# Top-k attention on one core: scores issued right behind the turned tiles, sums by transposes, and ScalarE's exponentials ahead of its evacuation

## The chip, the cores and the metric

One core of one Trainium2 chip runs the whole program. The metric is the device time in microseconds (us), the median of several executions. Five engines work side by side, each on its own list of instructions in order, and semaphores tie them together: TensorE (PE in the profile, its weight loads PEld), VectorE (DVE), ScalarE (ACT), GpSimd (POOL) and SyncE (SP, which starts the DMAs).

## The reference, cut to what matters

```python
# x: 32 batches of 256 tokens x 128 channels; 16 heads of 8 channels
xn = layernorm(x)
q, k, v = heads(xn @ Wqkv.T + bqkv)
q, k = layernorm(q, q_gamma, q_beta), layernorm(k, k_gamma, k_beta)
scores = q @ k.T / sqrt(8)                      # 256 x 256 for each head
aw = softmax(scores)
aws = aw * (aw >= 12th largest of the row)      # topk = int(256 * 0.05)
o_s = (aws / (aws.sum(-1) + 1e-8)) @ v
qf, kf = softmax(q), softmax(k)                 # over the 8 channels
o_l = qf @ (kf.T @ v) / (qf @ kf.sum(tokens) + 1e-6)
o = a * o_s + (1 - a) * o_l                     # a = sigmoid(alpha), one for each head
y = x + o @ Wproj.T + bproj + xn @ W[idx] + b[idx]
```

## The kernel before, in words

**Passes, slots and tiles.** The loop `iterations` makes 34 passes, `it` from -2 to 31, and in a steady pass works on several batches at once. A pass has eight slots, `u_` from 0 to 7, one for each unit of two heads. A unit has four tiles of 128 rows x 256 keys. "Slot 5" below is what an engine's list holds for `u_ == 5`.

**One unit's way.** PE writes a unit's scores into `score_ps` (two buffers) one slot ahead, in `scores(u_)`, for unit u+1. In slot u, DVE finds each row's eight largest (`top`, `largest`), POOL takes the largest away from them (`drop`), and ACT makes the exponentials of the four tiles (`e`, line 879, each followed by a read of the accumulator) and of the eight largest (`e8`, line 884). In slot u+1 DVE replaces those eight in `e` (`remove`, line 661, into `rest`) and finds the next eight (`following`, line 667, `next8`). In slot u+2 POOL and ACT make the masks `below` (POOL three tiles or four, ACT the rest, line 892). In slot u+4 PE turns the eight half tiles: one transpose of `e` and one product with `minus_huge` for each, sixteen instructions into `turn_ps` (`turn`, lines 1051 and 1052). ACT evacuates `turn_ps` with a Relu into `kept` (line 839). Every second slot PE multiplies two units' `kept` by the values (`product`, into `pv_ps`).

**Single buffers.** `turn_ps` is one buffer: `turn(u_)` waits until `kept` of the slot before has been made (`turn_copied`). `work_ps` and `pv_ps` are one bank each and pass through many hands: `work_ps` through qfT, kv, lin, the turned q and k (`w_qkT`), their two remainders (`part`, three bf16 parts), the values (`w_v`, line 1144), the turned xn and the projections q and k (`w_qk`, line 1156); `pv_ps` through the products, the sums, the turned output and the output projection (lines 1128 to 1131).

**Sums.** `sums()` in slot 5 of PE brings the 8 channels and the row's sum of each head together: `oT` (ACT's copy of the products, 32 rows for each head) is the stationary operand and `gather`, 36 columns of zeros and ones, the moving one, eight times; each of these fp32 products is two instructions in the trace. Then `eps_ident` times `z` adds 1e-8 of the full sum, once for each half of the tokens. ACT copies the result in slot 5 (line 908).

**The order in a slot** is written out by hand on every engine. On PE: `turn`, `product` (even slots), `sums` (slot 5), `early`, `scores`, `late`. `early` holds the qfT transposes (slot 0), the turned output (1), the output projection (3), the second remainder (5), the values (6) and w_qk (7). `late` holds kv (1), lin (2), w_qkT (3), the first remainder (4) and the turned xn (6). On ACT: `kept`, then the copies that others wait for (slot 1 rsqrt, 3 lin, 4 the first part, 6 `v_aug`, 7 `over_rec`), the exponentials with `e8`, the masks of two units earlier, and the other copies (0 and 4 `oT`, 4 and 5 the further parts, 7 `qk_sq` and `qk_raw`). On POOL, `drop` is first in a slot; behind it come the steps of q and k's normalisation and the masks.

Of the kernel before, what the change touches and what calls it, by code (L numbers as in the profile page):

```python
# [84 lines left out]
def build(nc, x, Wqkv, bqkv, q_gamma, q_beta, k_gamma, k_beta, alpha, Wproj, bproj, W, bW, logits, u, y):  # L85
# [15 lines left out]
    with ExitStack() as ctx:  # L101
# [13 lines left out]
        gather = sb("gather", [P, 4 * VA])  # L115
# [169 lines left out]
        def _(pool):  # L285
# [24 lines left out]
            used = gather[:].rearrange("p (j e) -> p j e", e=VA)  # L310
            select(used, ALU.not_equal, 1.0, 0, [[-VW, 4], [-1, VA]], 1, 7).then_inc(s["gather_ready"], 1)
            select(minus_one[:], ALU.not_equal, -1.0, 0, [[-1, P]], 1, 8).then_inc(s["gather_ready"], 1)
# [466 lines left out]
        def _(act):  # L779
# [48 lines left out]
            def body(it, par, xr):  # L828
                nxt = 1 - par
                for u_ in range(UNITS):  # L830
# [4 lines left out]
                    if exists(it if u_ >= 4 else it - 1):  # L835

                        wait(act, s["pv_ready"], it * QUADS + (u_ - 8) // 2 + 1)
                        act.wait_ge(s["turn_ready"], g - 3)
                        nc.scalar.activation(kept[:, u_ % 4], turn_ps[:], ACT.Relu).then_inc(s["turn_copied"], 1)  # L839
# [9 lines left out]
                    if u_ == 1 and exists(it - 2):  # L849
                        act.wait_ge(s["w_osT"], it - 1)  # L850
                        nc.scalar.copy(osT[:], pv_ps[:, 0:N]).then_inc(s["osT_copied"], 1)
# [34 lines left out]
                    if exists(it if u_ >= 2 else it - 1):  # L886

                        r = (u_ - 2) % RING
                        act.wait_ge(s["next_ready"], TILES * (g - 1))
                        for t in range(POOL_TILES[r], TILES):  # L890

                            nc.scalar.activation(below[:, r, t, :], e[:, r, t, :], ACT.Relu, scale=-1.0,  # L892
                                                 bias=next8[:, r, t, TOPK - 9:TOPK - 8]).then_inc(s["below_act"], 1)


# [9 lines left out]
                    if u_ == 5 and exists(it - 1):  # L905
                        act.wait_ge(s["w_turn"], it)
                        wait(act, s["osp_ready"], it - 1)
                        nc.scalar.copy(sums_sb.rearrange("p g e -> p (g e)"), pv_ps[:, 0:NT * H * VA]).then_inc(  # L908
                            s["sums_copied"], 1)
                    if u_ == 0 and exists(it):  # L910
# [40 lines left out]
                    if u_ == 7 and exists(it + 2):  # L951
# [5 lines left out]
                        nc.scalar.copy(qk_raw[:], work_ps[:]).then_inc(s["raw_ready"], 1)  # L957
                    if (it, u_) == (-2, 7):
# [403 lines left out]
```

## Time and profile before

| | us |
|---|---|
| median of 3 runs | 1219.39 |
| lowest, highest | 1219.28, 1228.09 |
| the profiled execution, its own time | 1222.3 |
| its span in the profile | 1220.5 |
| DVE busy in the span | 1151.5 |
| ACT busy | 1065.0 |
| PE busy | 1011.5 |
| POOL busy | 995.2 |

The span is from the first to the last instruction of the profiled execution; its own time is what the device took for it. The profiler's granted clock of PE has two levels here, 1.00 (2.4 GHz) and 0.50 (1.2 GHz), and its mean over the span is 0.962. An engine's busy time says how much work it has; what holds the end is seen from the waits of the engine with the most work.

### The profile page before, as it was taken

To read this page: it belongs to the slowest core of one execution; us is meant where nothing else is said; L and a number is where in the kernel's file an instruction comes from. 1 tells how busy PE (TensorE), PEld (TensorE's weight loads), DVE (VectorE), ACT (ScalarE), POOL (GpSimd) and SP (SyncE) were. 2 spreads that over 40 slices of the span, in tenths; PEclk is the share of its full clock that TensorE was granted. 3 is DMA by queue.
4 is the path that set the end of the run, shared out by engine and by line. 5 is a ranking of instruction groups with operands and counts; after the bars stand their busy time and mean duration, and the time that the engine had idled before them with its cause. 6 is when DMAs were issued, how large, how long until landed. Compare 5 with 4: busy or idle time off the path is not lost.

```text
span 1220.5 us, 34803 instructions
## 1 busy us (share of the span) xinstructions
PE 1011.5 (83%) x9381; PEld 707.2 (58%) x9412; DVE 1151.5 (94%) x4358; ACT 1065.0 (87%) x3474; POOL 995.2 (82%) x1972
## 2 busy tenths in 40 slices
PE   4578888888888888888888888888888888888888
PEld 1356556656556556556655656656556655656655
DVE  6999999999999999999999999999999999999994
ACT  3689898999989899998899989899989898989884
POOL 5688888888888888888888888888888888888863
PEclk9989999999999899999999999899999999999988
DMA  3122222122222122222122222122222122222110
GB/s 101 42 65 66 84 83 79 37 67 70 84 83 83 37 62 70 84 84 84 36 68 65 84 84 83 37 62 71 83 84 82 38 72 61 84 79 79 44 46 10
DMA packets 165126, 82.79 MB, mean 68 GB/s; under 512 B 7737, under 2 KB 164927, under 8 KB 164930
## 3 DMA queue, kind: packets, MB, share of 16 engines
q1 hardware_dynamic: 164658, 80.43, 22.8%
q8 instruction: 77, 1.26, 0.4%
q14 instruction: 119, 0.97, 0.3%
q10 hardware_dynamic: 272, 0.13, 0.0%
HBM read 42.78 MB, written 37.75 MB: 66 GB/s over the span
## 4 chain that ended last, share of the span: by engine, by line
POOL 32%; PE 27%; ACT 19%; issue 15%; DVE 5%; DMA 1%; DVEq 0%; POOLq 0%; ACTq 0%; SPq 0%
ACT e L879 12%; POOL gap L437 10%; POOL below L441 5%; PE turn_ps L1051 5%; PE pv_ps L1073 3%; POOL qkn L359 3%; PE work_ps L1156 3%; POOL qk_b L359 3%; PE pv_ps L1084 3%; DVE top L654 3%; PE turn_ps L1052 2%; POOL drop L412 2%; PE work_ps L1144 2%; PE work_ps L1187 2%; POOL sq_half L422 2%
## 5 line engine op out<-in xcount | busy, mean ns | idle before, releaser
L879 ACT ACTIVATE e<-score_ps,drop 128x256 f32<-128x256 f32 x1024 | 475.2, 495 | 31.1 <-POOL drop L412 30.9
L1051 PE MATMUL turn_ps<-ident,e 128*128 128x128 f32 x2016 | 401.9, 293 | 21.0 <-ACT part L863 17.5
L661 DVE MATCH_REPLACE8 rest<-e 128x256 f32<-128x256 f32 x1020 | 415.9, 412 | 0.0
L667 DVE MAX8 next<-rest 128x8 f32<-128x256 f32 x1020 | 410.4, 419 | 0.5 <-issue 0.3
L654 DVE MAX8 top<-score_ps 128x8 f32<-128x256 f32 x1024 | 362.0, 419 | 34.4 <-PE score_ps L1033 34.1
L1052 PE MATMUL turn_ps<-minus_huge,below 128*128 128x128 bf16 x2016 | 380.0, 226 | 0.0
L437 POOL TENSOR_SCALAR gap<-e,next 128x256 bf16<-128x256 f32 x794 | 368.9, 479 | 0.0
L1051 PEld LDWEIGHTS turn_ps<-ident,e 128*128 128x128 f32 x2016 | 296.8, 147 | 59.3 <-issue 21.7
L839 ACT ACTIVATE kept<-turn_ps 128x1024 f32<-128x1024 f32 x252 | 267.5, 1062 | 56.9 <-PE turn_ps L1052 56.9
L441 POOL TENSOR_SCALAR below<-gap 128x768 bf16<-128x768 bf16 (+1 forms) x254 | 216.7, 853 | 41.4 <-POOL gap L437 41.4
L879 ACT ACTIVATION_READ_ACCUMULATOR e<-score_ps,drop 128x1 f32 x1024 | 232.9, 227 | 0.0
L1052 PEld LDWEIGHTS turn_ps<-minus_huge,below 128*128 128x128 bf16 x2016 | 222.3, 110 | 0.7
L412 POOL TENSOR_TENSOR drop<-top 128x36 f32<-128x36 f32 x256 | 62.8, 245 | 132.0 <-DVE top L654 117.7
L1073 PE MATMUL pv_ps<-kept,v_aug 128*32 128x256 f32 x2000 | 142.2, 404 | 2.9 <-ACT over L908 2.2
L892 ACT ACTIVATE below<-e,next 128x256 bf16<-128x256 f32 x222 | 120.1, 541 | 0.0
L1033 PE MATMUL score_ps<-k_slots,q_slots 64*128 64x256 bf16 x1024 | 105.1, 283 | 11.8 <-issue 5.4
L661 DVE MATCH_VALUE_LOAD rest<-e 128x8 f32 x1020 | 80.1, 79 | 15.5 <-ACT e L884 15.4
L1084 PE MATMUL pv_ps<-gather,oT 128*128 128x36 f32 x496 | 61.7, 281 | 32.8 <-ACT oT L901 32.8
L1073 PEld LDWEIGHTS pv_ps<-kept,v_aug 128*32 128x32 f32 x2000 | 55.4, 114 | 50.2 <-issue 31.7
L1084 PEld LDWEIGHTS pv_ps<-gather,oT 128*128 128x128 f32 x496 | 58.1, 192 | 39.8 <-ACT oT L901 39.8
L1033 PEld LDWEIGHTS score_ps<-k_slots,q_slots 64*128 64x128 bf16 x1024 | 30.7, 95 | 69.3 <-issue 60.7
L884 ACT ACTIVATE e<-drop 128x32 f32<-128x32 f32 x256 | 67.2, 263 | 0.0
(229 smaller groups left out, 1439.6 us busy)
## 6 DMA issues: line engine op xcount, KB each, us to landing
part_slots<-part SPq DMA_DIRECT2D x128, 192.0 KB, 2.3
q_slots<-part_slots SPq DMA_DIRECT2D x64, 256.0 KB, 3.5
k_slots<-part_slots SPq DMA_DIRECT2D x64, 256.0 KB, 4.2
part_slots<-part SPq DMA_DIRECT2D x64, 128.0 KB, 1.9
x_sb<-in_L_attn_x SPq DMA_DIRECT2D x32, 128.0 KB, 4.0
x_res<-in_L_attn_x SPq DMA_DIRECT2D x32, 128.0 KB, 4.2
out_y<-out_sb SPq DMA_DIRECT2D x32, 128.0 KB, 4.4
w_ops<-in_L_ffn_W SPq DMA_DIRECT2D x1, 512.0 KB
```

The lines of the kernel that those rows point to most:

```text
L437: nc.gpsimd.tensor_scalar(gap[:, half, t, :], e[:, r, t, :], -1.0, next8[:, r, t, TOPK - 9:TOPK - 8], ALU.mult, ALU.add).then_inc(s["gap_s ...
L441: nc.gpsimd.tensor_scalar(below[:, r, 0:many], gap[:, half, 0:many], HUGE, 0.0, ALU.min, ALU.max).then_inc(s["below_pool"], many)
L654: nc.vector.max(top[:, q, t, 1:9], score_ps[:, q, t // 2, t % 2, :]).then_inc(s["top_ready"], 1)
L661: nc.vector.match_replace(rest[:, t, :], e8[:, (u_ - 1) % 2, t, :], e[:, (u_ - 1) % RING, t, :], REMOVED).then_inc(s["rest_ready"], 1)
L667: nc.vector.max(next8[:, (u_ - 1) % RING, t, :], rest[:, t, :]).then_inc(s["next_ready"], 1)
L839: nc.scalar.activation(kept[:, u_ % 4], turn_ps[:], ACT.Relu).then_inc(s["turn_copied"], 1)
L879: nc.scalar.activation(e[:, u_ % RING, t, :], score_ps[:, u_ % 2, t // 2, t % 2, :], ACT.Exp, bias=drop[:, u_ % 2, t, 0:1], accum_out=z[:, ...
L1033: last = mm(score_ps[:, v_ % 2, hh, nt, :], q_slots[rows, side, v_, nt * P:(nt + 1) * P], k_slots[rows, side, v_, :], start=True, stop=True)
L1051: mm(dst, e[:, r, t, keys], ident[:], start=True, stop=False, is_transpose=True)
L1052: last = mm(dst, below[:, r, t, keys], minus_huge[:], start=False, stop=True)
L1073: last = mm(pv_ps[32 * j:32 * (j + 1), half * N:(half + 1) * N], v_aug[:, side, mc, 4 * q + j, :], kept[:, v_ % 4, j % 2, mc, :], start=(m ...
L1084: mm(pv_ps[:, at:at + 4 * VA], oT[:, nxt, q // 2, 1 - q % 2, t * P:(t + 1) * P], gather[:], start=(t == 0 and q == 0), stop=False, skip_gr ...
```

## The change

Four edits, all in the order or the form of work; nothing else differs.

1. `sums()` becomes eight transposes with a permutation: `gather` grows from 36 to 128 columns, the spare 92 columns pick rows of `oT` that hold zeros, and the product with `gather` is issued with `is_transpose`. The two products with `eps_ident` (16 columns each) become one of 32. The tail's own sums change alike. POOL makes one more `affine_select` in the set-up.
2. PE's order in a slot: `scores` stands right behind `turn`, save that `product` stays ahead of it in slots 0 and 4, and `early` in slots 3, 5 and 6. `product` of slots 2 and 6, `sums`, and `early` of slots 0, 1 and 7 now come behind `scores`.
3. ACT's `kept` (with its wait for `turn`) moves behind the slot's exponentials and `e8`, and the copy of `osT` behind it. ACT's lines shift: exponentials 873, `e8` 878, `kept` 884.
4. ACT's masks `below` move from behind the exponentials to the end of the slot (line 956).

```diff
-        gather = sb("gather", [P, 4 * VA])
+        gather = sb("gather", [P, P])
...
-            used = gather[:].rearrange("p (j e) -> p j e", e=VA)
+            used = gather[:, 0:4 * VA].rearrange("p (j e) -> p j e", e=VA)
+            spare = gather[:, 4 * VA:].rearrange("p (j e) -> p j e", e=VW - VA)
             select(used, ALU.not_equal, 1.0, 0, [[-VW, 4], [-1, VA]], 1, 7).then_inc(s["gather_ready"], 1)
+            select(spare, ALU.not_equal, 1.0, -VA, [[-VW, 4], [-1, VW - VA]], 1, 7).then_inc(s["gather_ready"], 1)
...
-                    if exists(it if u_ >= 4 else it - 1):
-
-                        wait(act, s["pv_ready"], it * QUADS + (u_ - 8) // 2 + 1)
-                        act.wait_ge(s["turn_ready"], g - 3)
-                        nc.scalar.activation(kept[:, u_ % 4], turn_ps[:], ACT.Relu).then_inc(s["turn_copied"], 1)
...
                         nc.scalar.activation(e8[:, u_ % 2], drop[:, u_ % 2, :, 1:9], ACT.Exp).then_inc(s["e8_ready"], 1)
 
-                    if exists(it if u_ >= 2 else it - 1):
-
-                        r = (u_ - 2) % RING
-                        act.wait_ge(s["next_ready"], TILES * (g - 1))
-                        for t in range(POOL_TILES[r], TILES):
-
-                            nc.scalar.activation(below[:, r, t, :], e[:, r, t, :], ACT.Relu, scale=-1.0,
-                                                 bias=next8[:, r, t, TOPK - 9:TOPK - 8]).then_inc(s["below_act"], 1)
-
-
+                    if exists(it if u_ >= 4 else it - 1):
+
+                        wait(act, s["pv_ready"], it * QUADS + (u_ - 8) // 2 + 1)
+                        act.wait_ge(s["turn_ready"], g - 3)
+                        nc.scalar.activation(kept[:, u_ % 4], turn_ps[:], ACT.Relu).then_inc(s["turn_copied"], 1)
...
                         for q in range(QUADS):
                             at = (t * QUADS + q) * 4 * VA
-                            mm(pv_ps[:, at:at + 4 * VA], oT[:, nxt, q // 2, 1 - q % 2, t * P:(t + 1) * P], gather[:],
-                               start=(t == 0 and q == 0), stop=False, skip_group_check=True)
+                            mm(pv_ps[:, at:at + P], oT[:, nxt, q // 2, 1 - q % 2, t * P:(t + 1) * P], gather[:],
+                               start=(t == 0 and q == 0), stop=False, is_transpose=True, skip_group_check=True)
...
-                    for t in range(NT):
-                        over_t = pv_ps[:, t * H * VA:(t + 1) * H * VA].rearrange("p (h e) -> p h e", e=VA)[:, :, D]
-                        last = mm(over_t, eps_ident[:], z[:, nxt, t, :], start=False, stop=True, skip_group_check=True)
-                    last.then_inc(s["w_turn"], 1)
+                    mm(pv_ps[:, 0:NT * H * VA].rearrange("p (g e) -> p g e", e=VA)[:, :, D], eps_ident[:],
+                       z[:, nxt].rearrange("p t h -> p (t h)"), start=False, stop=True,
+                       skip_group_check=True).then_inc(s["w_turn"], 1)
...
                     if exists(it if u_ >= 4 else it - 1):
                         turn(u_)
-                    if u_ % 2 == 0 and exists(it if u_ >= 6 else it - 1):
+                    if u_ in (0, 4) and exists(it - 1):
                         product(u_)
+                    if u_ in (3, 5, 6) or u_ == 7 and it < 0:
+                        early(u_)
+                    if exists(it if u_ < UNITS - 1 else it + 1):
+                        scores(u_)
+                    if u_ in (2, 6) and exists(it if u_ >= 6 else it - 1):
+                        product(u_)
+                    if u_ == 0 or u_ == 7 and it >= 0:
+                        early(u_)
                     if u_ == 5 and exists(it - 1):
                         sums()
-                    early(u_)
-                    if exists(it if u_ < UNITS - 1 else it + 1):
-                        scores(u_)
                     late(u_)
+                    if u_ == 1:
+                        early(u_)
```

ACT, slots 1 to 3 of a steady pass, before: `kept` stands ahead of each slot's exponentials. The first row is the end of slot 1, the last one the end of slot 3's exponentials.

```order
L892 ACTIVATE below<-e,next 128x256
L839 ACTIVATE kept<-turn_ps 128x1024
L879 ACTIVATE e,z<-score_ps,drop 128x256 x4
L884 ACTIVATE e<-drop 128x32
L892 ACTIVATE below<-e,next 128x256
L839 ACTIVATE kept<-turn_ps 128x1024
L857 COPY over<-work_ps 128x288
L879 ACTIVATE e,z<-score_ps,drop 128x256 x4
L884 ACTIVATE e<-drop 128x32
```

The same stretch of the changed kernel, from the end of slot 1:

```order
L956 ACTIVATE below<-e,next 128x256
L873 ACTIVATE e,z<-score_ps,drop 128x256 x4
L878 ACTIVATE e<-drop 128x32
L884 ACTIVATE kept<-turn_ps 128x1024
L956 ACTIVATE below<-e,next 128x256
L851 COPY over<-work_ps 128x288
L873 ACTIVATE e,z<-score_ps,drop 128x256 x4
L878 ACTIVATE e<-drop 128x32
L884 ACTIVATE kept<-turn_ps 128x1024
```

Slot 2's `kept`, which stood ahead of slot 2's exponentials and of their wait for `drop`, now stands behind them.

PE, the end of slot 5's `turn` to the start of slot 6's, before:

```order
L1052 MATMUL turn_ps<-minus_huge,below 128x128
L1084 MATMUL pv_ps<-gather,oT 128x36 x8
L1090 MATMUL pv_ps<-z,eps_ident 128x16 x2
L1097 MATMUL work_ps<-part,minus_one 128x512
L1033 MATMUL score_ps<-k_slots,q_slots 128x256 x4
L1051 MATMUL turn_ps<-ident,e 128x128
```

and of the changed kernel:

```order
L1052 MATMUL turn_ps<-minus_huge,below 128x128
L1096 MATMUL work_ps<-part,minus_one 128x512
L1033 MATMUL score_ps<-k_slots,q_slots 128x256 x4
L1084 MATMUL pv_ps<-gather,oT 128x128 x8
L1088 MATMUL pv_ps<-z,eps_ident 128x32
L1051 MATMUL turn_ps<-ident,e 128x128
```

The sums, half as many instructions and wider ones, moved behind the scores; the remainder (`minus_one`) stays ahead of them.

PE, the end of slot 6's `turn` to the start of slot 7's, before:

```order
L1052 MATMUL turn_ps<-minus_huge,below 128x128
L1073 MATMUL pv_ps<-kept,v_aug 32x256 x8
L1144 MATMUL work_ps<-w_v,xnT 128x128
L1145 MATMUL work_ps<-bias,ones 128x128
L1144 MATMUL work_ps<-w_v,xnT 128x128
L1145 MATMUL work_ps<-bias,ones 128x128
L1033 MATMUL score_ps<-k_slots,q_slots 128x256 x4
L1213 MATMUL work_ps<-ident,xn 128x128 x2
```

and of the changed kernel:

```order
L1052 MATMUL turn_ps<-minus_huge,below 128x128
L1143 MATMUL work_ps<-w_v,xnT 128x128
L1144 MATMUL work_ps<-bias,ones 128x128
L1143 MATMUL work_ps<-w_v,xnT 128x128
L1144 MATMUL work_ps<-bias,ones 128x128
L1033 MATMUL score_ps<-k_slots,q_slots 128x256 x4
L1073 MATMUL pv_ps<-kept,v_aug 32x256 x8
L1212 MATMUL work_ps<-ident,xn 128x128 x2
```

The product moved behind the scores; the values stay ahead of them.

## Rows read from the trace of the kernel before

**Rows 1.** Stretches, one a pass: length; busy PE, PEld, DVE, ACT, POOL; PE's clock

```profile
30.98:66.72 35.74, 21.06 (x146) 13.27 (x148) 34.85 (x131) 25.56 (x95) 25.42 (x51) 1.00 0.21 61
...
615.58:651.02 35.44, 29.99 (x296) 21.35 (x295) 35.07 (x135) 33.02 (x109) 30.69 (x61) 1.00 0.23 66
...
1125.58:1163.01 37.43, 29.47 (x284) 20.77 (x283) 34.95 (x132) 33.71 (x111) 30.38 (x59) 0.93 0.25 71
```

**Rows 2.** Who waited for whom: us in total, times, longest us

```profile
ACT kept L839 <- PE turn_ps L1052: 56.9, 58, 7.3
DVE top L654 <- PE score_ps L1033: 34.1, 33, 5.5
DVE rest L661 <- ACT e L884: 15.4, 31, 0.6
```

**Rows 3.** DVE in time order: start us, us, line, operation [idle before]

```profile
610.66 1.43 DVE L654 MAX8 top<-score_ps 128x8 f32<-128x256 f32 x4 [0.99 <-PE score_ps L1033]
612.68 0.09 DVE L661 MATCH_VALUE_LOAD rest<-e 128x8 f32 x1 [0.59 <-ACT e L884]
...
624.50 1.41 DVE L654 MAX8 top<-score_ps 128x8 f32<-128x256 f32 x4
...
633.72 1.42 DVE L654 MAX8 top<-score_ps 128x8 f32<-128x256 f32 x4
...
637.92 1.42 DVE L654 MAX8 top<-score_ps 128x8 f32<-128x256 f32 x4
...
646.33 1.42 DVE L654 MAX8 top<-score_ps 128x8 f32<-128x256 f32 x4
```

**Rows 4.** Stretches with one slot's turned tiles alone, `turn_ps`, columns as in rows 1

```profile
604.80:607.75 2.95, 2.82 (x16) 2.02 (x16) 0.00 (x0) 0.00 (x0) 0.51 0.03 7
641.50:643.30 1.80, 1.59 (x16) 1.28 (x16) 0.00 (x0) 0.00 (x0) 1.00 0.02 6
```

**Rows 5.** PE in time order, turned tiles left out

```profile
601.98 1.98 PE L1084 MATMUL pv_ps<-gather,oT 128*128 128x36 f32 x16 [1.07 <-ACT oT L901]
...
610.08 0.40 PE L1033 MATMUL score_ps<-k_slots,q_slots 64*128 64x256 bf16 x4
...
628.93 0.44 PE L1128 MATMUL pv_ps<-x_res,ident 128*128 128x128 f32 x2
...
631.12 0.40 PE L1033 MATMUL score_ps<-k_slots,q_slots 64*128 64x256 bf16 x4
...
644.37 0.49 PE L1144 MATMUL work_ps<-w_v,xnT 128*128 128x128 f32 x2
...
645.52 0.40 PE L1033 MATMUL score_ps<-k_slots,q_slots 64*128 64x256 bf16 x4
```

**Rows 6.** ACT in time order, accumulator reads left out

```profile
616.29 0.65 ACT L953 ACTIVATE qk_sq<-work_ps 128x512 f32<-128x512 f32 x1
...
627.10 0.47 ACT L879 ACTIVATE e<-score_ps,drop 128x256 f32<-128x256 f32 x1 [0.50 <-POOL drop L412]
...
629.03 0.52 ACT L892 ACTIVATE below<-e,next 128x256 bf16<-128x256 f32 x1
629.43 1.03 ACT L839 ACTIVATE kept<-turn_ps 128x1024 f32<-128x1024 f32 x1
...
640.46 0.51 ACT L879 ACTIVATE e<-score_ps,drop 128x256 f32<-128x256 f32 x1
```

**Rows 7.** POOL in time order

```profile
617.39 0.73 POOL L422 TENSOR_TENSOR sq_half<-qk_sq 128x256 f32<-128x256 f32 x1
...
626.82 0.25 POOL L412 TENSOR_TENSOR drop<-top 128x36 f32<-128x36 f32 x1
```

**Rows 8.** Stretches, `work_ps` alone: w_qk of slot 7, columns as in rows 1

```profile
648.50:650.35 1.85, 1.75 (x6) 0.78 (x6) 0.00 (x0) 0.00 (x0) 1.00 0.99 263
```

**Rows 9.** Stretches, `pv_ps` alone: slot 1's four transposes; the sums (no DVE column)

```profile
621.20:622.00 0.80, 0.63 (x4) 0.42 (x4) 0.00 (x0) 1.00 0.00 0
638.70:641.20 2.50, 2.41 (x20) 2.31 (x20) 0.00 (x0) 1.00 0.40 123
```

More of the change, by code:

```diff
@@ L848, in body @@
                             s["over_ready"], 1)
-                    if u_ == 1 and exists(it - 2):
-                        act.wait_ge(s["w_osT"], it - 1)
-                        nc.scalar.copy(osT[:], pv_ps[:, 0:N]).then_inc(s["osT_copied"], 1)
                     if u_ == 1 and (exists(it + 1) or exists(it + 2)):
@@ L909, in body @@
                             s["sums_copied"], 1)
+                    if u_ == 1 and exists(it - 2):
+                        act.wait_ge(s["w_osT"], it - 1)
+                        nc.scalar.copy(osT[:], pv_ps[:, 0:N]).then_inc(s["osT_copied"], 1)
                     if u_ == 0 and exists(it):
@@ L957, in body @@
                         nc.scalar.copy(qk_raw[:], work_ps[:]).then_inc(s["raw_ready"], 1)
+                    if exists(it if u_ >= 2 else it - 1):
+                        r = (u_ - 2) % RING
+                        act.wait_ge(s["next_ready"], TILES * (g - 1))
+                        for t in range(POOL_TILES[r], TILES):
+                            nc.scalar.activation(below[:, r, t, :], e[:, r, t, :], ACT.Relu, scale=-1.0,
+                                                 bias=next8[:, r, t, TOPK - 9:TOPK - 8]).then_inc(s["below_act"], 1)
                     if (it, u_) == (-2, 7):
@@ L1152, in early @@
                             pe.wait_ge(s["pool_const"], 7)
-                            pe.wait_ge(s["gather_ready"], 3)
+                            pe.wait_ge(s["gather_ready"], 4)
                         for t in range(NT):
@@ L1321, in _ @@
             sums_ps = turn_ps[:, 0].rearrange("p m n -> p (m n)")
-            for t in range(NT):
-                over_t = sums_ps[:, t * H * VA:(t + 1) * H * VA].rearrange("p (h e) -> p h e", e=VA)[:, :, D]
-                mm(over_t, eps_ident[:], z[:, side, t, :], start=(t == 0), stop=False, skip_group_check=True)
+            mm(sums_ps[:, 0:NT * H * VA].rearrange("p (g e) -> p g e", e=VA)[:, :, D], eps_ident[:],
+               z[:, side].rearrange("p t h -> p (t h)"), start=True, stop=False, skip_group_check=True)
             for q in range(QUADS):
@@ L1328, in _ @@
                     at = (t * QUADS + q) * 4 * VA
-                    last = mm(sums_ps[:, at:at + 4 * VA], oT[:, side, q // 2, 1 - q % 2, t * P:(t + 1) * P], gather[:],
-                              start=False, stop=(q == QUADS - 1), skip_group_check=True)
+                    last = mm(sums_ps[:, at:at + P], oT[:, side, q // 2, 1 - q % 2, t * P:(t + 1) * P], gather[:],
+                              start=False, stop=(q == QUADS - 1), is_transpose=True, skip_group_check=True)
             last.then_inc(s["w_turn"], 1)
```

## The prediction

> **What bounds the kernel now.** I read the stretches of whole passes first. A pass here runs from DVE's first `top` of slot 0 to the next pass's. There are 31 of them, from 30.98 to 1163.01 us, so 36.52 us each on average [rows 1]. In the pass at 615.58 DVE is busy for 35.07 of 35.44 us: VectorE is the bound, and the rest of a pass is what DVE waits for. The clock column splits the passes in two kinds. Twelve of the 31 show 1.00, eight of those last 35.4 to 35.8 us and the longest 36.5; the other nineteen show 0.95 or less and last 36.3 to 38.5. Then the waits: in the whole run DVE waits 34.1 us for scores, once a pass, and 15.4 us for `e8`, 0.5 a pass [rows 2]. So 1.6 us a pass is all that a better order can remove, 49.5 us or 4% of the run, unless VectorE's own work shrinks, which the change leaves alone.
>
> Where are the waits? In the pass before the one at 615.58, at the start of slot 7: `top` waits 0.99 us for scores that ended at 610.48, and then `remove` 0.59 us for `e8` [rows 3, 5]. Ahead of this PE ran at half clock: slot 6's turned tiles took 2.82 us there against 1.59 us a pass later at full clock [rows 4], and in that later pass `top` of slot 7 started at 646.33 with no wait in its row [rows 3]. In seventeen of the nineteen passes the clock falls 2.1 to 4.1 us into slot 5, during or just behind the sums, which PE reaches after 1.07 us of idle time [rows 5], and comes back 3.4 us later, or 6.8 in three passes. So the waits for scores are mostly the price of the clock.
>
> **The sums.** Before, slot 5's sums take 2.41 us for 20 instructions [rows 9], all ahead of the scores for slot 6. Eight transposes with 128 columns are nearest to slot 1's four, which take 0.63 us with the tail of the last [rows 9]: about 1.1 us, and 0.2 us for the one product with `eps_ident`. As half of the instructions go, 2.41 us is the dear end and 1.1 the cheap one; I take 1.3. Neither is on DVE's path, since the sums now stand behind the scores and ACT's copy of them waits for `kept` anyway. What they may change is the clock. What PE does before it falls is the idle stretch and the narrow sums. Where it does a slot's turned tiles around an idle stretch, the clock holds, and turned tiles are themselves half transposes of 128 columns, as the new sums are. So I expect the clock to hold. A fall now costs more, see below.
>
> The Trainium skill speaks against this. "TensorE: Matmul & The Clock Gate", Part 4 on the PE-mode transpose, says that transposes do not count as busy for the clock. The trace rather disagrees, as the turned tiles are half transposes and keep 1.00. By that rule the falls would stay or spread, which is the second rival.
>
> **The scores behind the turned tiles.** In slots 6 and 2 the product (1.1 us) no longer stands ahead of the scores, in slot 5 the sums, in slot 0 qfT, in slot 1 the turned output, in slot 7 w_qk (1.75 us, [rows 8]). All of it is time by which scores could come earlier, if nothing else holds the turned tiles that stand in front of them.
>
> **`kept` behind the exponentials.** This is what holds them. `turn_ps` is one buffer, so slot u+1's turned tiles wait for slot u's `kept`. Before, `kept` waited for PE alone, and PE was the slower of the two (56.9 us of ACT waiting for turned tiles [rows 2]). Now `kept` also waits for slot u's exponentials, these for `drop`, this for DVE's `top`. This closes a loop over two slots: `top` of slot u, `drop`, exponentials, `kept`, `turn` of u+1, what stands between it and the scores, scores, `top` of slot u+2. Every time round it must fit into DVE's two slots. Its steps:
>
> - exponentials start 0.03 us after `drop`'s end (626.82+0.25, then 627.10), and the next ACT instruction behind `e8` starts 1.93 us later (629.03) [rows 6, 7];
> - `kept` takes 1.03 us [rows 6], the turned tiles 1.59 at full clock [rows 4], the scores 0.40 [rows 5]; from their end to `top` it is 0.18 us (610.48 to 610.66) [rows 3, 5]. For ACT to PE I estimate 0.05, and -0.15 for each group of PE that starts before the one ahead has ended.
>
> *Slot 2 to slot 4.* `drop` ends 2.57 us after slot 2's `top` starts (627.07-624.50), as POOL is behind there. Between `turn` and scores stands the output projection: 2.19 us from its start to the scores' (631.12-628.93) [rows 5]. Sum 2.57+0.03+1.93+1.03+0.05+1.59+2.19+0.40+0.18-0.15 = 9.8 us, against the 9.22 from `top` to `top` (633.72-624.50) [rows 3]: 0.6 us of new waiting at slot 4's `top`.
>
> *POOL on top of it.* w_qk is now behind slot 7's scores, so `qk_sq` (0.65 us, [rows 6]) ends at the earliest 1.75+0.65-0.2 = 2.2 us after slot 0's `top`. `sq_half` started at +1.81 before (617.39, `top` at 615.58) [rows 1, 7] and moves by 0.4. From there to slot 4 POOL has hardly a gap, so slot 2's `drop` comes up to 0.4 us later. Bounds 0 and 0.4; I take 0.4, as POOL is continuously at work there.
>
> *Slot 5 to slot 7.* Slot 4's work on ACT is the same sum in another order, so slot 5's exponentials start where they did, 2.54 us after `top` (640.46-637.92) [rows 3, 6]. Between `turn` and scores stand the values, 1.15 us (645.52-644.37) [rows 5]. Sum 2.54+1.93+1.03+0.05+1.59+1.15+0.40+0.18-0.15 = 8.7 us against 8.41 (646.33-637.92): 0.3 us at slot 7's `top`. `v_aug` and the exponentials of slot 6 wait for the same values, so `e8` is late by the full 0.59 us in every pass, as in each pass in which `top` waits now [rows 3].
>
> The other slots have no work between `turn` and scores or only 1.1 us (slot 4's product), and the same sum gives 7 to 8.3 us in 8.4 to 9 us. They have 0.1 to 1 us to spare, so I add 0.1 for the tightest, slot 1.
>
> **The masks** at the end of a slot are turned two slots later, and hold only ACT: nothing. The new `affine_select` stands in the first 31 us, where POOL waits for loads: nothing, at most the half microsecond that it takes. The tail saves some of its sums, below half a microsecond.
>
> **The sum.** A pass becomes 35.07 of DVE's work + 0.6 + 0.4 + 0.3 + 0.6 + 0.1 = 37.1 us, 0.55 more than the mean of 36.52, over some 30 passes +17 us. From the profiled execution (span 1220.5, own time 1222.3) that gives 1239, from the median of 1219.39, which is 3 us lower than that execution, **1236 us**. Each wait is a difference of two large sums, so its error is a few tenths: 0.5 us a pass either way is 15 us, and the forecast's own range is 1222 to 1250.
>
> **Rivals.** *The loop does not bind.* If `kept` is in time, because the chain from slot 2's `drop` to slot 4's `top` takes 9.2 us or less and the one of slot 5 8.4 or less, and the clock holds, every pass is one of 35.44 us or a little less: 1219-30x1.08 = 1187 us. For it: my two overruns are only 0.3 and 0.6 us, and waits shift other waits. Against it: `drop` of slot 2 is late by its own engine. It decides at about half a microsecond in each chain.
>
> *The clock still falls.* In nineteen of 31 passes, behind the sums. Then slot 6's turned tiles cost 2.82-1.59 = 1.23 us more, now fully on the loop, and the values a little, 1.4 together: 0.61x1.4x30 = 26 us on top of the forecast, 1262. If it falls in every pass, 1278. For it: PE has less work and more idle time, about 1 us ahead of most slots' turned tiles. Against it: slot 5's sums are as wide as turned tiles.
>
> *A draw.* The clock's gain and the loop's loss cancel: the waits move to other slots, passes last 36.5 us, 1219.
>
> **Chances.** The forecast 0.45, the loop does not bind 0.20, the clock falls 0.18, a draw 0.17. A change of 1% (1207 to 1232) is about what a measurement can tell from none. Of the forecast's 0.45 about 0.13 lies below 1232. Same: 0.13+0.15 and 0.02 of the first rival: 0.30. Faster: 0.18 and 0.02: 0.20. Slower: 0.32+0.18: 0.50. The range runs from 1190, next to the first rival, which keeps about half of its chance in, to 1266, with most of the second.
>
> **What the changed profile would show.** Right: DVE's `top` in slot 4 waits for scores behind the output projection, a wait that is not there now; PE's turned tiles wait for ACT's `kept` in most slots, where now ACT waits for PE; `e8` is waited for about 0.6 us a pass; PE's clock is near 1.00 in the steady passes. Wrong: waits for scores under 10 us in the whole run (then the loop does not bind), or clock falls behind slot 5's sums as before.

## The result, and the profile after

| | median us | lowest, highest | ratio to before, 95% interval |
|---|---|---|---|
| before, beside the changed kernel | 1221.86 | 1219.28, 1228.09 | |
| changed | 1251.56 | 1248.48, 1253.95 | 1.0234 [1.0185, 1.0283] |

The change makes the kernel 2.3% slower, about 30 us. The profiled execution took 1252.17 us and its span is 1250.3, against 1222.3 and 1220.5 before. The mean granted clock rose from 0.962 to 0.981, and yet the time rose.

The page of the changed kernel, its span, parts 1 and 2 (PE's clock in 40 slices), and the group of the moved `kept` from part 5:

```profile
span 1250.3 us, 34136 instructions
...
PE 952.4 (76%) x9061; PEld 657.8 (53%) x9092; DVE 1157.6 (93%) x4358; ACT 1074.7 (86%) x3474; POOL 1001.3 (80%) x1973
...
PEclk9989999999999999999999999999999999999998
...
L884 ACT ACTIVATE kept<-turn_ps 128x1024 f32<-128x1024 f32 x252 | 264.0, 1048 | 2.4 <-PE turn_ps L1052 2.4
```

DVE has the same 4358 instructions and nearly the same busy time (1157.6 us; 1151.5 before), PE is busy for 59 us less. So no engine has notably more to do; DVE waits more. The last number in `kept`'s row is the idle time ahead of it: 2.4 us in the whole run, where before it waited 56.9 us for turned tiles [rows 2]. ACT is hardly ever early with `kept` any more.

Stretches of single passes of the changed kernel, columns as in [rows 1]:

```profile
69.25:105.85 36.60, 26.38 (x266) 17.96 (x268) 35.24 (x135) 31.63 (x104) 30.56 (x61) 1.00 0.21 60
632.95:670.16 37.21, 28.75 (x284) 20.07 (x285) 35.44 (x135) 32.88 (x106) 30.63 (x61) 1.00 0.26 73
670.16:707.17 37.01, 28.78 (x284) 20.06 (x285) 35.34 (x136) 33.41 (x109) 31.09 (x62) 1.00 0.24 70
481.52:520.28 38.76, 30.16 (x284) 20.78 (x285) 35.47 (x135) 34.55 (x112) 31.59 (x62) 0.96 0.22 61
707.17:745.77 38.60, 28.84 (x284) 20.08 (x285) 35.36 (x136) 34.75 (x112) 31.54 (x62) 1.00 0.23 66
1157.36:1195.42 38.06, 29.60 (x281) 20.33 (x281) 35.04 (x131) 33.73 (x111) 30.27 (x58) 0.96 0.24 67
```

Nine of the thirty passes behind the first last 37.01 to 37.03 us, as the third row: that is the forecast's 37.1. But the mean of the thirty is (1195.42-69.25)/30 = 37.54, against 36.54 before ((1163.01-66.72)/30, [rows 1]): +1.00 a pass, 30 us in all. The first pass takes 38.41 us against 35.74, the tail 2.6 less; these two cancel. There are two kinds of longer passes: with a fall of the clock (0.96 in the fourth and the last row, nine passes), and with full clock and a long last slot (38.60, fifth row).

Who waited for whom in the changed kernel, us in total, times, longest:

```profile
PE turn_ps L1051 <- ACT kept L884: 255.0, 181, 2.4
...
DVE top L656 <- PE score_ps L1033: 49.8, 58, 2.7
...
DVE rest L663 <- ACT e L878: 18.3, 31, 0.6
...
PE score_ps L1033 <- issue: 8.5, 13, 1.5
```

PE now stands 255 us in front of turned tiles for `kept`; before, the wait ran the other way. DVE waits 49.8 us for scores (34.1 before, [rows 2]) and 18.3 for `e8` (15.4). The last row is the one that my prediction had no word for: PE stands at scores and "issue" names no releaser. The same view of the kernel before had it too, smaller:

```profile
PE score_ps L1033 <- issue: 5.4, 7, 1.2
```

The pass at 632.95, DVE in time order: `top` of slots 2, 3, 4, 5 and 7.

```profile
641.89 1.40 DVE L656 MAX8 top<-score_ps 128x8 f32<-128x256 f32 x4
...
652.15 1.61 DVE L656 MAX8 top<-score_ps 128x8 f32<-128x256 f32 x4 [0.96 <-PE score_ps L1033]
...
656.56 1.41 DVE L656 MAX8 top<-score_ps 128x8 f32<-128x256 f32 x4
...
665.18 1.43 DVE L656 MAX8 top<-score_ps 128x8 f32<-128x256 f32 x4
```

PE in the same pass, slot 3: turned tiles, output projection, scores.

```profile
647.98 0.30 PE L1051 MATMUL turn_ps<-ident,e 128*128 128x128 f32 x1 [0.70 <-ACT kept L884]
...
649.37 0.44 PE L1127 MATMUL pv_ps<-x_res,ident 128*128 128x128 f32 x2
...
651.57 0.40 PE L1033 MATMUL score_ps<-k_slots,q_slots 64*128 64x256 bf16 x4
```

ACT, slot 2 of the pass:

```profile
644.87 0.47 ACT L873 ACTIVATE e<-score_ps,drop 128x256 f32<-128x256 f32 x1 [0.63 <-POOL drop L414]
...
646.69 0.24 ACT L878 ACTIVATE e<-drop 128x32 f32<-128x32 f32 x1
646.81 1.03 ACT L884 ACTIVATE kept<-turn_ps 128x1024 f32<-128x1024 f32 x1
```

POOL, `qk_sq`'s half in slot 0 and `drop` of slot 2:

```profile
635.16 0.73 POOL L424 TENSOR_TENSOR sq_half<-qk_sq 128x256 f32<-128x256 f32 x1 [0.34 <-ACT qk_sq L945]
...
644.59 0.25 POOL L414 TENSOR_TENSOR drop<-top 128x36 f32<-128x36 f32 x1
```

Read as a chain: `top` 641.89, `drop` ends 644.84, exponentials to `e8`, `kept` 646.81 to 647.84, turned tiles from 647.98, scores from 651.57, `top` 652.15. That is 10.26 us from `top` to `top`, where DVE's own work took 9.22 before [rows 3].

Now the last slot of the long pass at 707.17. SP's queue, start and length of the issue, PE, and DVE's `top` of the next pass's slot 0:

```profile
740.78 0.36 SPq L272 DMA_DIRECT2D q_slots<-part_slots  x1
741.19 0.50 SPq L272 DMA_DIRECT2D k_slots<-part_slots  x1
```

```profile
742.11 0.30 PE L1051 MATMUL turn_ps<-ident,e 128*128 128x128 f32 x1 [1.72 <-ACT kept L884]
...
745.19 0.40 PE L1033 MATMUL score_ps<-k_slots,q_slots 64*128 64x256 bf16 x4 [1.53 <-issue]
```

```profile
745.77 0.43 DVE L656 MAX8 top<-score_ps 128x8 f32<-128x256 f32 x1 [1.56 <-PE score_ps L1033]
```

These scores are unit 0 of the next batch. Its q and k come through DRAM: ACT's third part (its copy ends at 736.76, 0.68 us from 736.08) is written out by SP, and when the writes have landed SP reads them back, q at 740.78 and k at 741.19. The reload takes 3.3 and 3.9 us from issue to landing (medians of 64). So k lands near 745.1, and PE, with the turned tiles done, stands 1.53 us for it. In thirteen of thirty passes PE waits here. What varies from pass to pass is mostly the write leg: the last write, issued 0.5 us behind the copy, lands 1.9 to 2.0 us after its issue in seventeen passes and 2.6 to 3.7 us after it in the other thirteen, and twelve of the thirteen waits follow such a late landing. Why it is late there was not looked into.

The clock of the changed kernel: slot 2 of the pass at 481.52, and the longest stretch without a fall.

```profile
492.45:495.87 3.42, 3.42 (x28) 2.11 (x30) 2.73 (x11) 2.79 (x11) 3.42 (x6) 0.50 0.00 0
495.87:1055.60 559.73, 429.70 (x4225) 299.53 (x4232) 527.74 (x1999) 498.06 (x1610) 462.74 (x911) 1.00 0.24 69
```

For 560 us, some fifteen passes and as many sums, the clock holds 1.00. It falls in nine passes, in slot 2, behind the turned output and an idle stretch in front of turned tiles, as PE's row just ahead of the fall shows (the idle time in brackets):

```profile
492.28 0.30 PE L1051 MATMUL turn_ps<-ident,e 128*128 128x128 f32 x1 [1.14 <-ACT kept L884]
```

### The profile page after: what moved, and what is told of

Read it like the earlier page. It is cut to its first block, busy times and chain, and to the rows that moved or that the text cites. A ratio compares the mean times of both kernels' runs of the same rounds, so it can differ in the third digit from the quotient of the medians.

```text
span 1250.3 us, 34136 instructions
## 1 busy us (share of the span) xinstructions
PE 952.4 (76%) x9061; PEld 657.8 (53%) x9092; DVE 1157.6 (93%) x4358; ACT 1074.7 (86%) x3474; POOL 1001.3 (80%) x1973
## 4 chain that ended last, share of the span: by engine, by line
ACT 37%; PE 31%; POOL 16%; issue 11%; DVE 5%; DVEq 0%; DMA 0%; POOLq 0%; ACTq 0%; SPq 0%
ACT e L873 18%; ACT kept L884 10%; PE turn_ps L1051 10%; POOL gap L439 5%; PE turn_ps L1052 4%; PE work_ps L1155 3%; POOL below L443 3%; DVE top L656 3%; PE score_ps L1033 2%; PE pv_ps L1130 2%; PE work_ps L1143 2%; POOL qk_a L355 2%; POOL drop L414 2%; ACT oT L890 1%; ACT qk_exp L915 1%
## 5 line engine op out<-in xcount | busy, mean ns | idle before, releaser
L1051 PE MATMUL turn_ps<-ident,e 128*128 128x128 f32 x2016 | 389.6, 287 | 255.1 <-ACT kept L884 255.0
L1051 PEld LDWEIGHTS turn_ps<-ident,e 128*128 128x128 f32 x2016 | 289.8, 144 | 310.3 <-issue 217.5
L656 DVE MAX8 top<-score_ps 128x8 f32<-128x256 f32 x1024 | 361.9, 415 | 53.8 <-PE score_ps L1033 49.8
L669 DVE MAX8 next<-rest 128x8 f32<-128x256 f32 x1020 | 405.7, 413 | 0.5 <-issue 0.3
L1052 PE MATMUL turn_ps<-minus_huge,below 128*128 128x128 bf16 x2016 | 369.5, 223 | 0.0
L873 ACT ACTIVATION_READ_ACCUMULATOR e<-score_ps,drop 128x1 f32 x1024 | 223.2, 218 | 0.0
L1052 PEld LDWEIGHTS turn_ps<-minus_huge,below 128*128 128x128 bf16 x2016 | 217.3, 108 | 0.0
L1073 PE MATMUL pv_ps<-kept,v_aug 128*32 128x256 f32 x2000 | 136.3, 391 | 0.0
L663 DVE MATCH_VALUE_LOAD rest<-e 128x8 f32 x1020 | 74.6, 73 | 18.3 <-ACT e L878 18.3
L861 ACT COPY v_aug<-work_ps 128x256 f32<-128x256 f32 x32 | 11.9, 373 | 51.6 <-PE work_ps L1144 51.6
L1155 PE MATMUL work_ps<-w_qk,xnT 128*128 128x256 f32 x128 | 46.9, 449 | 0.9 <-ACT xnT L942 0.9
```

The costliest lines, as they stand in the source:

```text
L656: nc.vector.max(top[:, q, t, 1:9], score_ps[:, q, t // 2, t % 2, :]).then_inc(s["top_ready"], 1)
L663: nc.vector.match_replace(rest[:, t, :], e8[:, (u_ - 1) % 2, t, :], e[:, (u_ - 1) % RING, t, :], REMOVED).then_inc(s["rest_ready"], 1)
L669: nc.vector.max(next8[:, (u_ - 1) % RING, t, :], rest[:, t, :]).then_inc(s["next_ready"], 1)
L873: nc.scalar.activation(e[:, u_ % RING, t, :], score_ps[:, u_ % 2, t // 2, t % 2, :], ACT.Exp, bias=drop[:, u_ % 2, t, 0:1], accum_out=z[:, ...
L1051: mm(dst, e[:, r, t, keys], ident[:], start=True, stop=False, is_transpose=True)
L1052: last = mm(dst, below[:, r, t, keys], minus_huge[:], start=False, stop=True)
```

## The experiments

"Per pass" is the mean of the thirty passes behind the first in the profiled execution, 36.54 us before and 37.54 changed. The ratio is always to the kernel before.

### The halves of the change

**ACT's new order alone**, on the kernel before (`kept` and the `osT` copy behind the exponentials, masks at the end of the slot):

```diff
-                    if exists(it if u_ >= 4 else it - 1):    # kept, ahead of the slot's copies and exponentials
...
                         nc.scalar.activation(e8[:, u_ % 2], drop[:, u_ % 2, :, 1:9], ACT.Exp)...
+                    if exists(it if u_ >= 4 else it - 1):    # kept, behind e8
```

> The kernel before with ScalarE's new order alone (kept behind the exponentials, masks last); TensorE's order and the sums as before. Theory 1: the same loop now also holds the sums (2.4 us), the products, the turned output and w_qk between turned tiles and scores, so slots 4 to 6, 6 to 0 and 0 to 2 overrun too: a pass of 39 us or more, 1290 to 1340 us. Theory 2 (loop harmless): within 1% of the kernel before or of the changed one, under 1255 us.

Measured 1359.63 us, 1.1115 [1.1083, 1.1146], 40.84 us a pass. Its waits:

```profile
PE turn_ps L1049 <- ACT kept L882: 245.9, 166, 3.1
...
DVE top L654 <- PE score_ps L1031: 153.7, 125, 3.3
```

The loop through `kept` binds wherever `early`, a product or the sums still stand between turned tiles and scores: four waits for scores a pass instead of one. 3.0 us a pass fall on `top` of slot 0 alone, behind w_qk. This half by itself costs 11%, more than the 1290 to 1340 us expected.

**The short sums alone**, on the kernel before:

```diff
+                            mm(pv_ps[:, at:at + P], oT[:, nxt, q // 2, 1 - q % 2, t * P:(t + 1) * P], gather[:],
+                               start=(t == 0 and q == 0), stop=False, is_transpose=True, skip_group_check=True)
...
+                    mm(pv_ps[:, 0:NT * H * VA].rearrange("p (g e) -> p g e", e=VA)[:, :, D], eps_ident[:],
+                       z[:, nxt].rearrange("p t h -> p (t h)"), start=False, stop=True,
```

> The kernel before with the short sums alone (eight transposes of 128 columns and one product with eps_ident). If the wide transposes hold TensorE's clock: no falls in slot 5, mean granted clock over 0.985, passes of 35.4 to 35.8 us, about 1190 us. If transposes do not hold it: clock near 0.96 as before and 1205 to 1220 us, only the instruction time gained.

Measured 1199.83 us, 0.9804 [0.9773, 0.9834], 36.08 us a pass. Page and waits:

```profile
PE 961.2 (80%) x9092; PEld 659.2 (55%) x9092; DVE 1151.0 (96%) x4358; ACT 1065.4 (89%) x3474; POOL 998.7 (83%) x1973
...
PEclk9989999999999999899999999999999999999999
...
DVE top L656 <- PE score_ps L1035: 14.7, 18, 2.7
PE score_ps L1035 <- issue: 12.2, 14, 1.4
```

The half-clock time goes from 95 to 48 us, no steady pass has a fall behind slot 5's sums, and the wait for scores goes from 34.1 [rows 2] to 14.7 us. So this edit is worth 2% by itself. It comes through the clock, as the prediction's section on the sums expected: the shortest pass is 35.50 us, no shorter than the 35.44 before, so the instruction time saved buys nothing in an undisturbed pass. The last row and `top` of slot 0 hold a second reading. With w_qk still ahead of unit 0's scores, PE waits for the reload in 14 passes, and `top` of slot 0 waits 0.30 us a pass, against 0.13 before. That is as much as in the changed kernel (0.30).

**All of the change but `kept`'s move**:

```diff
+                    if exists(it if u_ >= 4 else it - 1):    # kept first in ACT's slot, as before
...
-                    if exists(it if u_ >= 4 else it - 1):    # kept behind e8
```

> The changed kernel with ScalarE's evacuation (kept) back ahead of the exponentials; masks, osT copy, TensorE's order and the short sums stay as changed. Theory 1 (the evacuation behind the exponentials closes a loop over two slots that is longer than VectorE's two slots): the waits for scores in slot 4 (0.84 us a pass) and slot 7 go and e8 is waited for less than 0.3 us; a pass is 35.1 to 35.8 us, 1180 to 1200 us in all. Theory 2 (the loss is in the DMA reload of the slots, ahead of scores of unit 0, and in the clock falls of slot 2): the evacuation is innocent, the run stays at 1235 to 1255 us. Theory 3 (masks at the end of the slot are late for the turned tiles): stays above 1235 too.

Measured 1269.55 us, 1.0367 [1.0313, 1.0421], 38.43 us a pass: 70 us above theory 1, and of the wrong sign. It is above theory 2's range as well, and although theory 3 (the masks) only asked for more than 1235 us, the waits name something that none of the three held:

```profile
PE score_ps L1033 <- issue: 93.1, 31, 4.6
ACT qk_sq L945 <- PE work_ps L1158: 85.4, 32, 5.0
DVE top L656 <- PE score_ps L1033: 84.2, 51, 3.3
```

PE in slot 7 of one pass, turned tiles left out:

```profile
679.46 0.44 PE L1212 MATMUL work_ps<-ident,xn 128*128 128x128 f32 x2
...
684.42 0.40 PE L1033 MATMUL score_ps<-k_slots,q_slots 64*128 64x256 bf16 x4 [3.16 <-issue]
684.75 0.70 PE L1155 MATMUL work_ps<-w_qk,xnT 128*128 128x256 f32 x2
...
691.77 0.61 PE L1033 MATMUL score_ps<-k_slots,q_slots 64*128 64x256 bf16 x4
```

With `kept` early, the turned tiles are early, and PE reaches unit 0's scores 3 us before the reload has landed, in every pass (31 waits, 93.1 us). w_qk, the work with which PE filled this time before, is queued behind the wait. `qk_sq` waits for it and the clock falls behind the idle stretch (at half from 685.4 for 6.8 us), so that slot 1's scores come late too (691.77; DVE's `top` waits 2.75 us for them). In the changed kernel the same wait is 8.5 us instead of 93.1, since `kept` behind the exponentials delays the turned tiles: one cost of the change hides the other.

**All of the change but ACT's new order** (`kept`, the `osT` copy and the masks where they were):

```diff
+                    if exists(it if u_ >= 4 else it - 1):    # kept first
+                    if u_ == 1 and exists(it - 2):           # the osT copy ahead of the exponentials
+                    if exists(it if u_ >= 2 else it - 1):    # masks right behind e8
```

> The changed kernel with all of ScalarE's old order: kept first, masks behind the exponentials, osT copied ahead of slot 1's exponentials. Theory 1: fast again, 1180 to 1205 us, a little slower than kept_first, as the osT copy now waits for transposes that TensorE has behind scores and kv. If it equals kept_first within 0.5%, neither masks nor osT matter. Theory 2: 1235 to 1255 us.

Measured 1312.58 us, 1.0713 [1.067, 1.0757]. Outside both ranges again, with the same wait of PE at unit 0's scores. It is worse than the run above by 43 us. In its profile, read from an execution of 1328 us and so only as to what waits, the `osT` copy stands ahead of slot 1's exponentials and waits for the turned output, which PE's new order puts behind the scores and kv; `e8` of that slot comes late for DVE (56.8 us of waiting for `e8` in the whole run, 12.9 in the run above). The masks moved in the same run, so how the 43 us divide between them and the `osT` copy is not shown.

### Two single terms

**The output projection behind the scores in slot 3**, on the changed kernel:

```diff
-                    if u_ in (3, 5, 6) or u_ == 7 and it < 0:
+                    if u_ in (5, 6) or u_ == 7 and it < 0:
...
-                    if u_ == 0 or u_ == 7 and it >= 0:
+                    if u_ in (0, 3) or u_ == 7 and it >= 0:
```

> The changed kernel with the output projection of slot 3 moved behind the scores. Theory 1 (the loop from slot 2 to slot 4 overruns by what stands between turned tiles and scores): the 0.84 us a pass at slot 4's top goes; the projection now delays slot 4's turned tiles, so some 0.2 us come back at slot 5. A pass shorter by 0.5 to 0.85 us: 1225 to 1238 us. If that wait has another cause it stays, and the run is within 4 us of 1251.

Measured 1240.98 us, 1.0134 [1.0094, 1.0174]. The wait at `top` of slot 4 is gone, and the shortest pass is 36.50 us instead of 37.01: the chain of slot 2 was real, and binding for 0.5 us a pass. The mean pass is 37.33, a gain of only 0.21; the rest is given back at slots 7 and 0 (0.48 and 0.61 us a pass) and in falls of the clock. So the run ended just above the 1225 to 1238 us expected.

**The first reload split smaller**, on the changed kernel. `FIRST` is the number of units that the first pair of transfers brings:

```diff
-FIRST = 4
+FIRST = 2
```

> The changed kernel with the first reload of the slots cut from four units to two (FIRST = 2), so that scores of unit 0 wait for half the bytes. If the waits at slot 0's top (0.35 us a pass, 0 to 1.6) are the reload's: they go, or go in most passes, 10 to 14 us less, 1237 to 1242 us. If the landing is the same for half the bytes, or the cause is another: 1249 to 1253 us.

Measured 1243.94 us, 1.017 [1.0137, 1.0202]. The DMA view, KB each and median us from issue to landing:

```profile
q_slots<-part_slots SPq DMA_DIRECT2D x32, 128.0 KB, 2.1
k_slots<-part_slots SPq DMA_DIRECT2D x32, 128.0 KB, 2.3
```

`top` of slot 0 waits 0.05 us a pass instead of 0.30. So the unnamed wait at unit 0's scores is the reload. But the pass is 37.45, hardly less, and the time just above the range expected: the clock now falls in slot 2 in nineteen passes (70 us at half clock in the whole run, 50 in the changed kernel), and `top` of slot 3 waits 0.38 us a pass instead of 0.22.

### The reload and w_qk

**w_qk back ahead of unit 0's scores**, `kept` still first (the third run with one more edit):

```diff
-                    if u_ in (3, 5, 6) or u_ == 7 and it < 0:
+                    if u_ in (3, 5, 6, 7):
...
-                    if u_ == 0 or u_ == 7 and it >= 0:
+                    if u_ == 0:
```

> kept_first (evacuation ahead of the exponentials, TensorE's new order) with w_qk of slot 7 back ahead of the scores of unit 0. Theory: kept_first lost because TensorE stood 3 us a pass at unit 0's scores, waiting for the reload of the slots with w_qk queued behind it, after which the clock fell. With w_qk ahead the idle stretch is filled: no falls in slot 7 or 0, waits at slot 1's top gone, passes of 35.2 to 35.8 us, 1183 to 1200 us. If the scores' new place itself is what hurts, it stays above 1225.

Measured 1199.19 us, 0.9787 [0.9745, 0.9829]. The place of w_qk alone takes off 70 us from the 1269.55. The waits at slot 1's top are gone, as expected, but nine passes still have a fall in slot 7 or 0. The wait for the reload is 1.4 us a pass on average instead of 3.0:

```profile
PE score_ps L1033 <- issue: 42.0, 31, 2.9
```

**The same with `FIRST = 2`:**

> kept_wqk with FIRST = 2 as well. If what is left at slot 0's top is the reload's landing: 5 to 12 us below kept_wqk, 1172 to 1190 us; else equal to it.

Measured 1175.45 us, 0.9604 [0.9572, 0.9636], 35.22 us a pass.

```profile
PE 948.2 (81%) x9092; PEld 658.5 (56%) x9092; DVE 1146.2 (98%) x4358; ACT 1068.6 (91%) x3474; POOL 998.4 (85%) x1973
...
DVE top L656 <- PE score_ps L1033: 7.6, 9, 2.7
```

DVE is busy for 98% of the span. The gain over the run above, 24 us by the medians, is more than the 5 to 12 expected; `top` of slot 0, DVE's only wait for scores left, goes from 0.67 to 0.17 us a pass, and the clock from 0.983 to 0.992.

**w_qk back ahead in the changed kernel**, with `kept` late:

> The changed kernel with w_qk of slot 7 back ahead of the scores of unit 0, nothing else. Theory 1: in the changed kernel the chain from slot 6 over kept to slot 0's top has no slack, so w_qk's 1.75 us land on it; they replace the wait for the reload (0.3 us a pass), so a pass gets 1.2 to 1.6 us longer: 1285 to 1300 us. If w_qk behind the scores were what costs the changed kernel its time, as it did with the evacuation first, it gets faster: under 1235 us.

Measured 1275.51 us, 1.0453 [1.0419, 1.0487], 38.34 us a pass, `top` of slot 0 waiting 1.62 us: the sign of theory 1, the size below its range. PE never stands for the reload at unit 0's scores here. With `kept` late, w_qk ahead of the scores costs 24 us; with `kept` first it gains 70. The same edit has both signs, and what decides, as the waits show it, is whether PE arrives there late, held by `kept`, or early, ahead of the reload.

**Short sums and `FIRST = 2` on the kernel before:**

> The kernel before with the short sums and the first reload cut to two units; both engines' orders as before. The reload's waits at slot 0's top (0.3 us a pass in sums_only) go: 1186 to 1194 us. What then is left to kept_wqk_first2's 1175 is what TensorE's new order without slot 7's part, and the masks' place, are worth: 11 to 19 us. If 1199 as sums_only, the reload is not what slot 0 waits for here.

Measured 1185.82 us, 0.9718 [0.968, 0.9755], 35.61 us a pass. So of the 4.0% of the version above, 2.8% need no new order at all; PE's new order and the masks at the end of ACT's slot add 10 us together, a little less than the 11 to 19 expected.

**The masks back behind `e8`**, in the version of 1175.45:

```diff
                         nc.scalar.activation(e8[:, u_ % 2], drop[:, u_ % 2, :, 1:9], ACT.Exp)...
+                    if exists(it if u_ >= 2 else it - 1):    # masks here, and not at the end of the slot
```

> kept_wqk_first2 with the masks back right behind the exponentials and e8. If the masks at the end of a slot help, by making the copies that others wait for 0.4 us earlier in each slot: 2 to 8 us slower, 1177 to 1184. If their place is nothing, as predicted for the change: 1175 within 2 us.

Measured 1193.46 us, 0.9771 [0.9733, 0.9808]. The masks at the end are worth 18 us there, which I had put at nothing; without them PE's new order is no gain over the run above (1185.82). Two things make `top` of slot 0 wait 0.68 us a pass instead of 0.17. ACT's third part is now copied behind the masks: its copy ends 5.8 to 6.0 us after slot 5's `top` instead of 5.4, and the reload is later by as much. And the clock falls in slot 6 in fourteen passes, where in the version of 1175.45 it falls in none: PE waits for the third part ahead of the values, and the half clock then makes it late. In twelve of the passes with such a wait the reload has landed 0.3 us or more before PE reaches unit 0's scores, without standing idle in front of them. One of these passes:

```profile
416.76 0.49 PE L1144 MATMUL work_ps<-w_v,xnT 128*128 128x128 f32 x2 [1.27 <-ACT part L919]
...
418.45 1.93 PE L1074 MATMUL pv_ps<-kept,v_aug 128*32 128x256 f32 x16
...
424.07 0.39 PE L1034 MATMUL score_ps<-k_slots,q_slots 64*128 64x256 bf16 x4
```

The product of slot 6 (1.93 us) takes 1.07 us at full clock.

**`FIRST = 1`**, in the version of 1175.45:

> kept_wqk_first2 with the first reload cut to one unit. The waits at slot 0's top (0.17 us a pass) go, but the seven other units' reload, 448 KB for each side, has one slot less until scores of unit 1 need it. Between 1170 and 1176 us if it lands in time, 1180 or more if slot 1 now waits for it.

Measured 1171.26 us, 0.9597 [0.9566, 0.9627], 35.12 us a pass.

```profile
DVE top L656 <- PE score_ps L1033: 4.4, 4, 2.7
```

The waits at slot 0's top shrink further, but the time against the kernel before, measured beside each, is the same as with `FIRST = 2` within the intervals (0.9597 and 0.9604): a gain from the last halving is not shown. This is the fastest version that ran: short sums, PE's new order save w_qk, ACT's masks at the end, `kept` first as before, and the first reload of one unit. It is 4.0% faster than the kernel before and 6.4% than the changed one (1171.26/1251.56).

## Why the prediction was right or wrong

The direction was right and the time inside the stated range, the size was not: the change forecast is about +14 to +17 us, the measured one +30, just above the forecast's own 1222 to 1250. A draw is excluded by the interval. By its own steps:

- *The sums*: right, 1.09 us for the eight transposes and 0.31 for the product with `eps_ident`, some 1.2 together (forecast 1.3), and the clock holds behind them (the 560 us stretch, and the short sums alone). The rival in which the clock still falls behind the sums is refuted for this kernel. "I expect the clock to hold" was right for slot 5 only: falls came in slot 2, in nine passes.
- *Slot 2 to slot 4 with POOL*: forecast 9.8+0.4 = 10.2, traced 10.26. `drop` ends 2.95 us after `top` (forecast 2.97), `sq_half` starts 2.21 us into the pass (forecast 2.2), turned tiles start 0.14 us after `kept`'s end (estimate 0.05). The run with the output projection moved confirms the term: 0.5 us on the shortest pass.
- *Slot 5 to slot 7*: forecast 8.7, traced 8.62 (665.18-656.56). `e8` 0.60 us a pass, as forecast.
- *The base pass*: forecast 37.1, and nine passes last 37.01 to 37.03. The signs named for "right" all came, and none of them could show what was left out.
- *"The masks ... nothing"*: wrong. In the version of 1175.45 us their place is worth 18 us, through ACT's copy of the third part, the reload and falls in slot 6. In the changed kernel itself this share was not measured.
- A reading: of the falls of 6.8 us before, two are in slot 5, not three; the others are in slots 3 and 7. Nothing hangs on it.

**The step that failed** is "The sum": 35.07+0.6+0.4+0.3+0.6+0.1 has no term for the reload in front of unit 0's scores and none for falls of the clock. The reload was left out without a reason, the falls on the argument about the sums alone. The omission starts in "The scores behind the turned tiles", which lets the scores come earlier "if nothing else holds the turned tiles": I followed only `turn_ps` and `kept`, and not the other thing that unit 0's scores wait for, the reload through SP's queue. The 1.00 us a pass splits so:

| | us a pass | us in 30 passes |
|---|---|---|
| base pass, 37.02-36.54 (forecast: +0.55) | 0.48 | 14.4 |
| passes without a fall above the base, 37.35-37.02 | 0.33 | 10 |
| passes with a fall above the others, 9 x 0.62 | 0.19 | 5.6 |

The second row is the reload: in the 21 passes without a fall, the waits at the `top` that ends the pass sum to 6.4 of the 7.0 us above the base. Over all thirty it is 0.30 us a pass, and 0.05 with the smaller first transfer. That this makes the kernel only 8 us faster, because more falls come in its place, was measured but not foreseen.

It is not w_qk's new place that brings this wait into the changed kernel. Before, with w_qk ahead, PE already stood for the reload in seven passes, and with the short sums alone, w_qk still ahead, `top` of slot 0 waits the same 0.30 us. My reading, which no run isolates, is that the waits at slot 7's top (0.57 us a pass before, 0.03 with the short sums) used to cover the landing. What w_qk's place decides is what stands behind the wait once `kept` is early.

Why an idle stretch of 1.1 us in slot 2 is followed by a fall in nine passes and not in the others stays open: the stretch is 1.14 us in most passes of either kind, the runs show the falls moving with the order around it, and no run varied this stretch alone.

The rival "the loop does not bind" was further off than its price: where `kept` does not wait for the exponentials, the kernel with PE's new order is 3.7% slower than before, as PE stands at the reload. A saving of that order appears only with w_qk back ahead of the scores (0.979), and fully with a smaller first transfer (0.960).

## What to carry to other kernels

- Before you move a consumer ahead of filler work on an in-order engine, list everything it waits for, the DMA chain behind its operands too, and when each lands. The filler that you move behind it is then queued behind that wait, with all that waits for the filler: w_qk ahead of or behind one group of scores was 70 us with `kept` early, and 24 us the other way with `kept` late.
- An edit in two halves has to be priced in each half. Here the sums alone gain 2.0%, ACT's order alone costs 11%, PE's order without ACT's costs 7.1% with the sums in it (3.7% where only `kept` stays first), and the edit of ACT is what hides most of that.
- Size a first transfer by what its first consumer needs: with nothing else changed, from four units to two took off 24 us where this wait was the last one in the way, 14 us with the short sums alone and 8 us in the changed kernel. From two to one no gain is shown.

## What the runs showed of the hardware

*Transposes and the clock.* The clock held 1.00 for 560 us over some fifteen passes in which half of the instructions for turned tiles and eight of ten for the sums are transposes, and the falls in slot 5 went away when the old sums became fewer and wider instructions, most of them transposes. The Trainium skill, "TensorE: Matmul & The Clock Gate", Part 4 on the PE-mode transpose, says that the full clock does not engage for transposes, which do not count as busy in the same way; by that rule the falls would have stayed. The measurement decides for this mix of work. It is no test of transposes alone: the edit changed form, width and number together, and falls do come elsewhere, in slot 2 behind four transposes and 1.14 us of idle time, where the same stretch also passes without one.

*The reload.* The same pair of transfers from DRAM takes, q and k, 1.8 and 2.0 us for 64 KB, 2.1 and 2.3 for 128, 3.3 and 3.9 for 256, 3.8 and 4.6 for 384. "DMA: Bandwidth & Descriptors" of the Trainium skill, section on the anatomy of one DMA, gives a fixed 2.0 us and the bytes at 436 GB/s on top, fitted on transfers that GpSimd issues. These here are SyncE's. A fixed part of about 2 us agrees with the smallest of them. The growth does not: from 64 to 256 KB q takes 1.5 us more, some 130 GB/s, with the k transfer running beside it. So a first transfer of 128 KB instead of 256 lands 1.2 us (q) and 1.6 us (k) sooner.

*The time of an fp32 instruction.* An fp32 product is two instructions in the trace and an fp32 transpose one. The sixteen instructions of the old sums, 36 columns wide, took 1.98 us [rows 5], 0.124 each; the eight transposes take 1.09, 0.136 each with 128 columns. So here the count of instructions set the time, and the columns, up to 128, hardly did, though a product and a transpose are compared. With 256 columns they do: one product of w_qk, two instructions, takes 0.70 us in the rows above. The new sums:

```profile
659.38 1.09 PE L1084 MATMUL pv_ps<-gather,oT 128*128 128x128 f32 x8
660.31 0.31 PE L1088 MATMUL pv_ps<-z,eps_ident 128*128 128x32 f32 x2
```
